# Preln attention on one Trainium2 core: q and k halves copied inside SBUF, chunks placed by hand, three denominator terms, loops written out

## The chip, the cores and the metric

The kernel runs on one core of one Trainium2 chip. The metric is device time in microseconds, from one launch to its end. PE is the tensor engine, DVE the vector engine, ACT the scalar engine, POOL GpSimd, and SP the engine that issues all of this kernel's DMAs.

## What is computed

Eight graphs of 1024 nodes with 512 features; 16 heads of 32.

```python
h = jnp.maximum(_layernorm(x, axis=-1), 0.0)
q, k, v = heads(h @ Wq + bq), heads(h @ Wk + bk), heads(h @ Wv + bv)
scores = jnp.einsum('bhqd,bhkd->bhqk', q, k) * scale
scores = jnp.where(adj[:, None] == 0, -jnp.inf, scores)
attn = jax.nn.softmax(scores, axis=-1)
out = jnp.einsum('bhqk,bhkd->bhqd', attn, v)
x = x + merged(out) @ Wo + bo
```

## The kernel before

A **unit** is four heads (128 of the 512 columns) of one graph; there are four units per graph and 32 in all. A unit has two **sweeps**, each over 512 queries. A sweep has 16 **steps**: eight tiles of 128 keys (kt) by two pairs of heads. So a unit has steps 0 to 31, and "step (2, 19)" is step 19 of a graph's unit 2.

For each step (function `scores`, line 681) PE multiplies a stacked k against a stacked q: q and k are kept as sums of two fp16 halves, high and low, and the four 32-row quarters of a 128-row operand hold (high, low, high, low) of q and (high, high, low, low) of k. One matmul of 128 rows so gives all four products of a head. A step's two score matmuls ("a score pair") are issued one step ahead into one of two pairs of PSUM banks. DVE subtracts the mask into a slot of `ring` (line 905), ACT takes the exponential in place (line 770). `ring` holds four key tiles.

Behind that PE runs **blocks** of four heads, each head on 32 columns of the array: `weighted` (line 694) adds a key tile's probabilities times v to the output (p0 to p7), `denominators` (line 705) adds up the softmax denominators in terms. POOL (`sums`, line 1079) first adds key tiles in pairs and threes into `acc`: kt 0, 1, 2 make term A, kt 3, 4, 5 term B. Key tiles 6 and 7 are terms of their own, straight from `ring`. The table `BLOCKS` says behind which step's scores which blocks stand; numbers of 16 and over run over into the next sweep.

In the space left, PE computes what later units and graphs need, in **chunks** of products that share two PSUM banks in turn: q and k for the next unit (12 products of 512 columns each, line 654), v (48 of 128 columns, line 661), the output projection y of the graph before (12, line 668), the transposes t of the next graph's normalised rows (4, line 650) and the row norms n (line 664) for a check of the fast path. `spread_out` deals a unit's chunks evenly over the steps without blocks, by a cost per product, so a step may end one chunk and begin the next. A chunk's bank is read by ACT (`high`, line 782, after the step in which its products end, then `square`) and by DVE (`low`, line 918, two steps after; `output` for y, `largest_norms` for n).

q's and k's halves lie in `part`. To become stacked operands they go through DRAM: `store_parts` (line 508) writes `part` to `parts`, and `load_stack` (line 513) waits for that and reads it back with four DMAs, one for each quarter, with all four heads.

On ACT, besides: `reciprocal` of the denominators (lines 798, 800, after step 2), `o_high`, `normalise` (line 819) and `to_mask` (line 825). On DVE: `scale_o`, `o_low` (line 960), `statistic` and others. POOL also adds the output bias to x (`bias_x`, line 1087). Each engine's program is written out for graph 0, runs in a hardware loop (`Fori`) over graphs 1 to 6, and is written out for graph 7. Waits are on counts that grow over the whole run. `general_attention` is a second path for other inputs, not run here.

## Time and profile before

| | |
|---|---|
| median of 3 runs | 2086.84 us (2086.14 to 2088.18) |
| the profiled execution | 2085.51 us |
| its span, first to last instruction | 2083.6 us |
| instructions | 40441 |
| PE clock granted, mean | 0.989 of 2.4 GHz |
| DMA | 206.61 MB in 103222 packets |

Times in the rows are microseconds from the start of the span, unless a row says ns. A matmul's end is modelled, so two that follow each other overlap in the timeline; the pitch from start to start is what one costs. "idle before <- X" names what ended an idle time. "x4" means four merged instructions. The chain follows the last instruction back, each time to what released it.

### The profile page before, as it was taken

To read this page: it belongs to the slowest core of one execution; us is meant where nothing else is said; L and a number is where in the kernel's file an instruction comes from. 1 tells how busy PE (TensorE), PEld (TensorE's weight loads), DVE (VectorE), ACT (ScalarE), POOL (GpSimd) and SP (SyncE) were. 2 spreads that over 40 slices of the span, in tenths; PEclk is the share of its full clock that TensorE was granted. 3 is DMA by queue.
4 is the path that set the end of the run, shared out by engine and by line. 5 is a ranking of instruction groups with operands and counts; after the bars stand their busy time and mean duration, and the time that the engine had idled before them with its cause. 6 is when DMAs were issued, how large, how long until landed. Compare 5 with 4: busy or idle time off the path is not lost.

```text
span 2083.6 us, 40441 instructions
## 1 busy us (share of the span) xinstructions
PE 1932.5 (93%) x14336; PEld 776.5 (37%) x14336; DVE 1557.3 (75%) x1587; ACT 1478.1 (71%) x1765; POOL 1302.1 (62%) x581
## 2 busy tenths in 40 slices
PE   3799899998999999999999999999899998999977
PEld 2334344343344333443334333334333343444312
DVE  5688777878768787687867877778767787767773
ACT  3577786677867788668876778767777677866672
POOL 0377567556666567656667557666557566676574
PEclk8999999999999999999999999999999999999999
DMA  5433244342444324343351434424234332442302
GB/s 177 122 87 96 82 112 132 88 107 64 120 112 124 83 76 132 86 122 86 92 142 56 115 93 117 119 74 119 81 109 122 88 106 66 117 122 64 74 1 81
DMA packets 103222, 206.61 MB, mean 99 GB/s; under 512 B 11616, under 2 KB 11744, under 8 KB 103008
## 3 DMA queue, kind: packets, MB, share of 16 engines
q1 hardware_dynamic: 103008, 203.80, 35.2%
q8 instruction: 129, 2.11, 0.4%
...
## 4 chain that ended last, share of the span: by engine, by line
PE 76%; DVE 7%; issue 6%; DMA 5%; ACT 2%; POOL 1%; SPq 1%; DVEq 0%; ACTq 0%; POOLq 0%
PE ps L694 20%; PE ps L681 19%; PE ps L654 15%; PE ps L705 10%; PE ps L668 7%; PE ps L661 6%; DVE ring L905 4%; DMA k_stack<-k_parts 2%; DMA k_parts<-k_part 1%; SPq L513 1%; DMA edges<-adjT 1%; ACT hT_hi L776 1%; DVE k_part L918 1%; POOL acc L1079 1%; ACT ring L770 1%
## 5 line engine op out<-in xcount | busy, mean ns | idle before, releaser
L905 DVE TENSOR_TENSOR ring<-ps,mask 128x1024 f32<-128x1024 f32 x1024 | 1234.6, 1219 | 435.7 <-PE ps L681 399.9
L770 ACT ACTIVATE ring<-ring 128x1024 f32<-128x1024 f32 x1024 | 1069.7, 1051 | 382.9 <-DVE ring L905 374.6
L1079 POOL TENSOR_TENSOR acc<-ring 128x1024 f32<-128x1024 f32 x256 | 604.1, 2371 | 730.2 <-ACT ring L770 729.4
L681 PE MATMUL ps<-q_stack,k_stack 128*128 128x512 f16 x2048 | 610.4, 382 | 85.2 <-DVE ring L905 61.4
L1079 POOL TENSOR_TENSOR acc<-acc,ring 128x1024 f32<-128x1024 f32 x256 | 617.6, 2432 | 0.0
L694 PE MATMUL ps<-ring,v_sb 128*32 128x512 f32 x4096 | 509.1, 604 | 0.0
L681 PEld LDWEIGHTS ps<-q_stack,k_stack 128*128 128x128 f16 x2048 | 157.1, 98 | 481.8 <-DVE ring L905 246.4
L694 PEld LDWEIGHTS ps<-ring,v_sb 128*32 128x32 f32 x4096 | 100.9, 109 | 252.3 <-issue 218.1
L705 PE MATMUL ps<-acc,ones 128*32 128x512 f32 x1024 | 139.8, 597 | 2.7 <-issue 2.6
L705 PE MATMUL ps<-ring,ones 128*32 128x512 f32 x1024 | 137.3, 592 | 0.0
L661 PE MATMUL ps<-wv_hi,hT_hi 128*128 128x128 f16 x1024 | 103.1, 219 | 3.2 <-DVE k_part L918 3.2
L661 PE MATMUL ps<-wv_lo,hT_hi 128*128 128x128 f16 x1024 | 103.2, 219 | 0.0
L825 ACT ACTIVATE mask<-edges,big 128x512 bf16<-128x512 uint32 x120 | 85.4, 711 | 23.1 <-DMA edges<-adjT 23.1
L661 PE MATMUL ps<-wv_hi,hT_lo 128*128 128x128 f16 x1024 | 100.8, 219 | 0.0
L1087 POOL TENSOR_TENSOR x_in<-x_in,bo_row 128x512 f32<-128x512 f32 x56 | 77.7, 1403 | 22.8 <-DMA x_in<-x 22.8
L798 ACT ACTIVATE rden<-ps 128x512 f32<-128x512 f32 x64 | 38.2, 597 | 68.9 <-PE ps L705 68.9
L654 PE MATMUL ps<-hT_hi,wq_hi 128*128 128x512 f16 x256 | 72.7, 388 | 14.2 <-DVE hT_lo L914 14.2
L661 PEld LDWEIGHTS ps<-wv_hi,hT_hi 128*128 128x128 f16 x1024 | 71.4, 98 | 21.9 <-DVE k_part L918 4.2
L668 PE MATMUL ps<-wo_hi,oT_hi 128*128 128x512 f16 x256 | 70.1, 383 | 9.6 <-DVE k_part L918 5.0
L661 PEld LDWEIGHTS ps<-wv_lo,hT_hi 128*128 128x128 f16 x1024 | 71.0, 98 | 14.2
L654 PE MATMUL ps<-hT_hi,wk_hi 128*128 128x512 f16 x256 | 72.5, 379 | 2.1 <-DVE q_part L918 2.1
L654 PE MATMUL ps<-hT_lo,wq_hi 128*128 128x512 f16 x256 | 74.1, 383 | 0.0
...
## 6 DMA issues: line engine op xcount, KB each, us to landing
...
edges<-adjT SPq DMA_DIRECT2D x128, 256.0 KB, 2.9
q_stack<-q_parts SPq DMA_DIRECT2D x128, 256.0 KB, 4.9
k_stack<-k_parts SPq DMA_DIRECT2D x128, 256.0 KB, 5.0
...
```

The lines of the kernel that those rows point to most:

```text
L654: i = nc.tensor.matmul(bank, w[WQ if kind == "q" else WK][:, c, cols], h[:, c, t * HALF:(t + 1) * HALF], start=m == 0, stop=m == 3 * DC - 1)
L661: i = nc.tensor.matmul(bank[:, tt * P:(tt + 1) * P], h[:, c, tok], w[WV][:, c, cols], start=km == 0, stop=km == 3 * DC - 1)
L668: i = nc.tensor.matmul(bank, o[:, c, t * P:(t + 1) * P], w[WO][:, c, :], start=m == 0, stop=m == 3 * DC - 1)
L681: i = nc.tensor.matmul(ps_s(j)[:, hh, :], stack["k"][:, up % 2, h, kt * P:(kt + 1) * P], stack["q"][:, up % 2, h, half * HALF:(half + 1) * ...
L694: i = nc.tensor.matmul(ps[h * DH:(h + 1) * DH, BANK_O, :], v_sb[:, up % 2, kt, h * DH:(h + 1) * DH], head_of(ring[:, slot_of(kt, h // 2), ...
L705: i = nc.tensor.matmul(ps[h * DH:(h + 1) * DH, BANK_D, :], ones[:], head_of(tile, h), start=term == TERMS[0], stop=term == TERMS[-1], tile ...
L770: nc.scalar.activation(tile, tile, ACT.Exp, scale=SCALE / UP / UP).then_inc(s["prob_ready"], 1)
L798: nc.scalar.activation(rden[:], ps[:, BANK_D, :], ACT.Ln).then_inc(s["ln_done"], 1)
L825: nc.scalar.activation(mask[:, kt, half * HALF:(half + 1) * HALF], edges[:, i % EDGE_SLOTS, :].bitcast(U32), ACT.Relu, bias=big[:], scale= ...
L905: nc.vector.tensor_tensor(ring[:, slot_of(kt, pair), :].rearrange("p (a n) -> p a n", n=HALF), ps_s(j), mask[:, kt:kt + 1, half * HALF:(ha ...
L1079: nc.gpsimd.tensor_tensor(acc[:, group, pair, :], first_of, ring[:, slot_of(kt, pair), :], ALU.add).then_inc(s["sum_done"], 1)
L1087: nc.gpsimd.tensor_tensor(tile, tile, bo_row[:], ALU.add).then_inc(s["x_biased"], 1)
```

## The change

1. **Copies.** `parts`, `store_parts` and `load_stack` are gone. `stack_part` copies one half (high or low) of q or k from `part` into the stack with eight DMAs inside SBUF, each of 32 rows of 1024 fp16 values: four heads by two quarters. The high halves are copied once ACT has written both, the low ones once DVE has. Each kind and half has its own semaphore, which ACT and DVE also wait for before they write the next unit's half.
2. **Chunks.** `spread_out` over all chunks is replaced by a table `PRODUCTS`: for each unit, chunk and kind, its first and last step. Only a few steps still hold products of two chunks. The tables `HIGH_AFTER`, `SQUARE_AFTER` and `LOW_AFTER` give for each chunk how many steps after its last product ACT and DVE read it. Statistics, normalising, the biases, masks, `o_high` and `o_low` get new steps; the reciprocal moves from step 2 to 3, `scale_o` from 4 to 5. The last chunk of unit 0 (n) ends in the first step of unit 1.
3. **Terms.** POOL adds kt 0, 1, 2, 3 to term A and 4, 5, 6 to term B; key tile 7 stays a term. There are three terms and ten additions per sweep, where there were four and eight. `BLOCKS` has four groups instead of five.
4. **No loops.** Graphs 1 to 6 are written out on every engine, with constants in the waits.
5. DVE waits for a graph's masks one key tile at a time, where it waited for eight at the head of a sweep.

```diff
-BLOCKS = {6: ("p0", "p1"), 10: ("p2", "p3", "dA"), 14: ("p4", "p5"), 16: ("p6", "dB", "d6"), 18: ("p7", "d7")}
-TERMS = "AB67"
+BLOCKS = {6: ("p0", "p1"), 10: ("p2", "p3"), 14: ("p4", "p5", "dA"), 18: ("p6", "dB", "p7", "d7")}
+TERMS = "AB7"
+SUMMED = {1: 0, 2: 2, 3: 4, 5: 6, 6: 8}
+SUMS = 10
+SUMMED_AT = {"A": 6, "B": 10}
...
-STATS_AT = {(1, 13): 0, (1, 17): 1, (1, 20): 2, (1, 23): 3, (1, 24): 4, (1, 25): 5, (1, 27): 6, (1, 29): 7}
-MEANS_AT, RSTD_AT, SHIFT_AT = (1, 31), (2, 1), (2, 3)
-NORMALISE_AT = {(2, 5): 0, (2, 7): 1, (2, 9): 2, (2, 11): 3, (2, 23): 4, (2, 25): 5, (2, 27): 6, (2, 29): 7}
-T_AT = {(2, 19): 0, (2, 21): 1, (2, 23): 2, (2, 25): 3, (2, 27): 4, (2, 29): 5, (3, 1): 6, (3, 3): 7}
...
+PRODUCTS = [
+    {("q", 0): (0, 3), ("q", 1): (4, 5), ("k", 0): (7, 8), ("k", 1): (8, 11), ("y", 0): (12, 13), ("y", 1): (15, 16), ("v", 0): (17, 20), ("y", 2): (22, 22), ("y", 3): (24, 24), ("y", 4): (26, 28), ("v", 1): (29, 31), ("n", 0): (32, 32)},
...
+LOW_AFTER = [
+    {("q", 0): 2, ("q", 1): 3, ("k", 0): 1, ("k", 1): 2, ("y", 0): 1, ("y", 1): 1, ("y", 2): 1, ("y", 3): 1, ("y", 4): 1, ("n", 0): 1},
...
+STATS_AT = {(1, 13): 0, (1, 18): 1, (1, 21): 2, (1, 23): 3, (1, 25): 4, (1, 27): 5, (1, 28): 6, (1, 30): 7}
+MEANS_AT, RSTD_AT, SHIFT_AT = (1, 31), (2, 0), (2, 4)
+NORMALISE_AT = {(2, 5): 0, (2, 7): 1, (2, 9): 2, (2, 11): 3, (2, 19): 4, (2, 25): 5, (2, 30): 6, (3, 6): 7}
+BIAS_AT = {(0, 4): 0, (0, 7): 1, (0, 10): 2, (0, 11): 3, (0, 22): 4, (0, 26): 5, (0, 30): 6, (1, 1): 7}
+MASK_AT = {3: [17, 18, 21, 22, 24, 26, 28, 30], 0: [1, 3, 5, 7, 8, 9, 10, 12]}
+
+RECIPROCAL_AT, SCALE_O_AT = 3, 5
+O_HIGH_AT, O_LOW_AT = [4, 17, 5, 5], [7, 19, 13, 7]
...
-def spread_out(chunks, slots):
-
-    total = sum(PIECES[kind] * COST[kind] for kind, _ in chunks)
-    plan, spent = {}, 0
-    for kind, t in chunks:
-        for piece in range(PIECES[kind]):
-            runs = plan.setdefault(slots[len(slots) * spent // total], [])
-            if runs and runs[-1][:2] == (kind, t):
-                runs[-1] = (kind, t, runs[-1][2], piece + 1)
-            else:
-                runs.append((kind, t, piece, piece + 1))
-            spent += COST[kind]
+def spread_out(chunk, slots):
+
+    n = PIECES[chunk[2]]
+    cuts = [n * i // len(slots) for i in range(len(slots) + 1)]
+    return {at: (*chunk, a, z) for at, a, z in zip(slots, cuts, cuts[1:]) if a < z}
+
+def chunk_plan():
+
+
+    plan = {}
+    for b in range(B):
+        for up in range(UNITS):
+            for (kind, t), (a, z) in PRODUCTS[up].items():
+                if kind == "y" and b == 0 or b == B - 1 and (kind == "t" or up == UNITS - 1):
+                    continue
+                slots = [j for j in range(a, z + 1) if j % SWEEP not in BUSY] or [a]
+                for at, run in spread_out((b, up, kind, t), [(b * UNITS + up) * TILES + j for j in slots]).items():
+                    plan.setdefault(at, []).append(run)
     return plan
...
-            def store_parts(kind):
-                sp.dma_start(parts[kind], part[kind][:]).then_inc(s[kind + "_stored"], 16)
-
-            def load_stack(U, parity, kind):
-                sp.wait_ge(s[kind + "_stored"], 16 * (U + 1))
-                for quarter, hl in enumerate({"q": (0, 1, 0, 1), "k": (0, 0, 1, 1)}[kind]):
-                    sp.dma_start(stack[kind][quarter * DH:(quarter + 1) * DH, parity, :, :],
-                                 parts[kind][:, hl, :].rearrange("(h p) n -> p h n", h=HG)).then_inc(s["stack_loaded"], 16)
+            def stack_part(U, parity, kind, hl):
+
+                for h in range(HG):
+                    for quarter, which in enumerate({"q": (0, 1, 0, 1), "k": (0, 0, 1, 1)}[kind]):
+                        if which == hl:
+                            sp.dma_start(stack[kind][quarter * DH:(quarter + 1) * DH, parity, h, :], part[kind][h * DH:(h + 1) * DH, hl, :])\
+                                .then_inc(s[f"{kind}_{('high', 'low')[hl]}_stacked"], 16)
 
...
-                        for kind, t in ending_at(up, first, last, j - 3, "qk"):
+                        for c in [c for c in HIGH_AT.get(G - 2, ()) if c[2] in "qk"]:
+                            g, u, kind, t = c
                             if t == 1:
-                                sp.wait_ge(s["low_ready"], chunk_no(SPLIT, b, up, first, (kind, t)) + 1)
-                                store_parts(kind)
-                        for kind, t in ending_at(up, first, last, j - 4, "y"):
-                            sp.wait_ge(stored[t % X_SLOTS], 16 * ((b - 1) * (QT // X_SLOTS) + t // X_SLOTS + 1))
+                                sp.wait_ge(s["high_ready"], chunk_no(SPLIT, c) + 1)
+                                stack_part(unit_no(g, u) + 1, (u + 1) % 2, kind, 0)
+                        for c in [c for c in LOW_AT.get(G - 1, ()) if c[2] in "qk"]:
+                            g, u, kind, t = c
+                            if t == 1:
+                                sp.wait_ge(s["low_ready"], chunk_no(SPLIT, c) + 1)
+                                stack_part(unit_no(g, u) + 1, (u + 1) % 2, kind, 1)
+                        for g, _, kind, t in [c for c in LOW_AT.get(G - 3, ()) if c[2] == "y"]:
...
-            with sp.Fori(1, B - 1) as b:
+            for b in range(1, B - 1):
...
-                    pe.wait_ge(s["stack_loaded"], STACKED * (U + 1))
+                    for kind in "qk":
+                        pe.wait_ge(s[f"{kind}_high_stacked"], STACKED * (U + 1))
+                        pe.wait_ge(s[f"{kind}_low_stacked"], STACKED * (U + 1))
...
-                    if stored_before is not None:
-                        act.wait_ge(s[kind + "_stored"], stored_before)
+                    if stacked_before is not None:
+                        act.wait_ge(s[kind + "_high_stacked"], stacked_before)
...
-                if kt < RING_KT:
-                    if not very_first:
-                        if kt < 2:
-                            dve.wait_ge(s["pv_done"], 8 * V + kt - 3)
-                            dve.wait_ge(s["sum_done"], 8 * V + 2 * kt - 3 + pair)
-                        else:
-                            dve.wait_ge(s["den_done"], len(TERMS) * V + kt - 3)
-                else:
-                    dve.wait_ge(s["pv_done"], 8 * V + kt - 3)
-                    dve.wait_ge(s["sum_done"], 8 * V + {4: 1, 5: 1, 6: 3, 7: 5}[kt] + pair)
+                before = (V - 1, kt + QT - RING_KT) if kt < RING_KT else (V, kt - RING_KT)
+                if not (kt < RING_KT and very_first):
+                    W, k = before
+                    dve.wait_ge(s["pv_done"], QT * W + k + 1)
+                    if k == QT - 1:
+                        dve.wait_ge(s["den_done"], len(TERMS) * (W + 1))
+                    else:
+                        dve.wait_ge(s["sum_done"], SUMS * W + SUMMED[k if k in SUMMED else k + 1] + pair + 1)
...
+                    if stacked_before is not None:
+                        dve.wait_ge(s[kind + "_low_stacked"], stacked_before)
...
-                        if up == 0 and j % SWEEP == 0:
-                            dve.wait_ge(s["mask_ready"], b * 2 * QT + QT * (j // SWEEP + 1))
+                        if up == 0 and j % PAIRS == 0:
+                            dve.wait_ge(s["mask_ready"], b * 2 * QT + j // PAIRS + 1)
...
-                group, k = divmod(kt, 3)
+                group, n = kt // 4, SUMS * V + SUMMED[kt] + pair
                 pool.wait_ge(s["prob_ready"], U * TILES + j + 1)
-                if k == 1 and pair == 0 and not very_first:
+                begins = kt % 4 == 1
+                if begins and pair == 0 and not very_first:
                     pool.wait_ge(s["den_done"], len(TERMS) * (V - 1) + group + 1)
-                if k == 2:
-                    pool.wait_ge(s["sum_done"], 8 * V + 4 * group + pair + 1)
-                first_of = ring[:, slot_of(kt - 1, pair), :] if k == 1 else acc[:, group, pair, :]
+                if not begins:
+                    pool.wait_ge(s["sum_done"], n - 1)
+                first_of = ring[:, slot_of(kt - 1, pair), :] if begins else acc[:, group, pair, :]
```

How the order moves at three places. **PE, graph 0, steps 15 to 19.** L681 (L688 in the change) is a score pair, L694 (L701) four heads' weighted sums with 4 per block, L705 (L712) four heads' denominator term, from `acc` or `ring`; L654 and L661 (L659 and L666) are products for q, k and v. Before:

```order
L681 MATMUL ps<-q_stack,k_stack 128x512 x2
L694 MATMUL ps<-ring,v_sb 32x512 x4
L705 MATMUL ps<-acc,ones 32x512 x4
L705 MATMUL ps<-ring,ones 32x512 x4
L681 MATMUL ps<-q_stack,k_stack 128x512 x2
L654 MATMUL ps<-hT_lo,wk_hi 128x512 x3
L654 MATMUL ps<-hT_hi,wk_lo 128x512
L681 MATMUL ps<-q_stack,k_stack 128x512 x2
L694 MATMUL ps<-ring,v_sb 32x512 x4
L705 MATMUL ps<-ring,ones 32x512 x4
L681 MATMUL ps<-q_stack,k_stack 128x512 x2
```

Now:

```order
L688 MATMUL ps<-q_stack,k_stack 128x512 x6
L666 MATMUL ps<-wv_hi,hT_hi 128x128 x4
L666 MATMUL ps<-wv_lo,hT_hi 128x128 x4
L666 MATMUL ps<-wv_hi,hT_lo 128x128 x4
L666 MATMUL ps<-wv_hi,hT_hi 128x128 x4
L688 MATMUL ps<-q_stack,k_stack 128x512 x2
L701 MATMUL ps<-ring,v_sb 32x512 x4
L712 MATMUL ps<-acc,ones 32x512 x4
L701 MATMUL ps<-ring,v_sb 32x512 x4
L712 MATMUL ps<-ring,ones 32x512 x4
L688 MATMUL ps<-q_stack,k_stack 128x512 x2
```

A group of three blocks (p6, B, 6) and, two steps on, one of two (p7, 7) have become one of four (p6, B, p7, 7); the products of a step are now all of one chunk.

**POOL, graph 0, first additions.** Before, then now:

```order
L1079 TENSOR_TENSOR acc<-ring 128x1024 x2
L1079 TENSOR_TENSOR acc<-acc,ring 128x1024 x2
L1079 TENSOR_TENSOR acc<-ring 128x1024 x2
L1079 TENSOR_TENSOR acc<-acc,ring 128x1024 x2
L1079 TENSOR_TENSOR acc<-ring 128x1024 x2
L1079 TENSOR_TENSOR acc<-acc,ring 128x1024 x2
```

```order
L1087 TENSOR_TENSOR acc<-ring 128x1024 x2
L1087 TENSOR_TENSOR acc<-acc,ring 128x1024 x4
L1087 TENSOR_TENSOR acc<-ring 128x1024 x2
L1087 TENSOR_TENSOR acc<-acc,ring 128x1024 x2
L1087 TENSOR_TENSOR acc<-ring 128x1024 x2
L1087 TENSOR_TENSOR acc<-acc,ring 128x1024 x4
```

Before, a pair of additions that start a sum is followed by one pair that adds to it. Now two pairs follow for term A, one for term B.

**SP, graph 0, from the edges of its second half-masks on.** Before, then now:

```order
L519 DMA edges<-adjT 128x512 x8
L508 DMA q_parts<-q_part 128x2048
L513 DMA q_stack<-q_parts 32x4x1024 x4
L508 DMA k_parts<-k_part 128x2048
L513 DMA k_stack<-k_parts 32x4x1024 x4
```

```order
L518 DMA edges<-adjT 128x512 x5
L512 DMA q_stack<-q_part 32x1024 x8
L518 DMA edges<-adjT 128x512
L512 DMA q_stack<-q_part 32x1024 x8
L518 DMA edges<-adjT 128x512 x2
L512 DMA k_stack<-k_part 32x1024 x16
```

A store and four loads per kind have become sixteen copies, in two eights, and edge loads now stand between them and behind them.

## Rows read from the trace of the kernel before

**Rows 1.** The page, parts 1 and 4: busy us, share, instructions; the chain by engine.
```profile
PE 1932.5 (93%) x14336; PEld 776.5 (37%) x14336; DVE 1557.3 (75%) x1587; ACT 1478.1 (71%) x1765; POOL 1302.1 (62%) x581
...
PE 76%; DVE 7%; issue 6%; DMA 5%; ACT 2%; POOL 1%; SPq 1%; DVEq 0%; ACTq 0%; POOLq 0%
```

**Rows 2.** The chain in order of time, middle of unit 3 to 0: start, us, what.
```profile
688.44 0.43 PE ps L681 x2
688.87 1.29 PE ps L654 x6
```

**Rows 3.** Busy time by engine (instructions): graph 4's first sweep, its sixth, the whole.
```profile
1051.20:1087.30 36.10, 34.52 (x196) 11.91 (x197) 25.97 (x23) 27.68 (x36) 24.59 (x12) 1.00 0.43 120
...
1214.00:1244.20 30.20, 25.18 (x214) 10.31 (x210) 23.43 (x24) 22.50 (x28) 18.74 (x8) 1.00 0.34 87
1051.20:1301.90 250.70, 239.68 (x1792) 96.55 (x1792) 191.57 (x194) 184.50 (x223) 162.85 (x72) 1.00 0.37 102
```

**Rows 4.** The chain again: three blocks, two blocks, the score pair behind, products for v.
```profile
679.56 1.00 PE ps L694 x8
680.56 1.72 PE ps L705 x16
...
692.33 1.85 PE ps L694 x16
694.18 0.54 PE ps L681 x2
...
706.65 1.28 PE ps L661 x23
```

**Rows 5.** PE's timeline in unit 2's second sweep: start, us, line, idle before it.
```profile
983.12 0.60 PE L681 MATMUL ps<-q_stack,k_stack 128*128 128x512 f16 x2 [1.26 <-DVE ring L905]
```

**Rows 6.** POOL's lines 1079 and 1087, one by one: ns min/median/max.
```profile
L1079 POOL TENSOR_TENSOR acc<-acc,ring x256: 2340/2372/3436, 79.5 to 2042.7; 128x1024 f32<-128x1024 f32 x128
...
L1087 POOL TENSOR_TENSOR x_in<-x_in,bo_row x56: 1264/1282/2264, 314.6 to 1869.2; 128x512 f32<-128x512 f32 x56
```

**Rows 7.** PE's timeline at the back edge into graph 4, and out of the loop.
```profile
1048.82 0.61 PE L681 MATMUL ps<-q_stack,k_stack 128*128 128x512 f16 x2
1051.25 0.60 PE L681 MATMUL ps<-q_stack,k_stack 128*128 128x512 f16 x2 [1.83 <-issue]
...
1054.28 0.63 PE L705 MATMUL ps<-acc,ones 128*32 128x512 f32 x3 [0.59 <-issue]
...
1056.12 0.60 PE L681 MATMUL ps<-q_stack,k_stack 128*128 128x512 f16 x2
...
1803.71 1.04 PE L681 MATMUL ps<-q_stack,k_stack 128*128 128x512 f16 x4
...
1807.39 0.61 PE L681 MATMUL ps<-q_stack,k_stack 128*128 128x512 f16 x2
```

**Rows 8.** SP's issues and PE before the first scores.
```profile
49.72 0.33 SPq L508 DMA_DIRECT2D q_parts<-q_part  x1
...
54.89 0.35 SPq L508 DMA_DIRECT2D k_parts<-k_part  x1
...
68.55 1.86 PE L681 MATMUL ps<-q_stack,k_stack 128*128 128x512 f16 x4 [9.45 <-DMA k_stack<-k_parts]
```

**Rows 9.** Lines 513 and 519: issue of stack loads in ns; landing of edge loads.
```profile
L513 SPq DMA_DIRECT2D k_stack<-k_parts x128: 302/432/1437, 61.1 to 1967.7; - x128
...
DMA to landing us min/median/max: 2.4/2.9/7.2
```

**Rows 10.** DVE's line 960, then DVE and POOL at 562 to 568.
```profile
L960 DVE SCALAR_TENSOR_TENSOR oT_lo<-o_raw,b_up,oT_hi x32: 1273/1341/3482, 137.9 to 2052.0; 128x1024 f16<-128x1024 f32 x32
...
564.77 3.13 DVE L960 SCALAR_TENSOR_TENSOR oT_lo<-o_raw,b_up,oT_hi 128x1024 f16<-128x1024 f32 x1
...
562.11 4.71 POOL L1079 TENSOR_TENSOR acc<-acc,ring 128x1024 f32<-128x1024 f32 x2
```

**Rows 11.** Waits: who waited for whom, us in total, times, longest.
```profile
DVE ring L905 <- ACT mask L825: 15.5, 6, 3.3
```

More of the change, by code:

```diff
@@ L267 @@
 UP = 64.0
-STACKED = 16 * 2 * P // DH
+STACKED = 16 * HG * 2
 RING_KT = 4
@@ L753, in _ @@
             graph(0, True, False)
-            with pe.Fori(1, B - 1) as b:
+            for b in range(1, B - 1):
                 graph(b, False, False)
```

204 lines of the change are left out of this document (85 added, 119 removed), and 14 rows, old and new, of tables (HIGH_AFTER, LOW_AFTER, PRODUCTS, SQUARE_AFTER).

## The prediction

> **What bounds the kernel now.** I read the page's busy shares and its chain first [rows 1]: PE 93%, DVE 75%, ACT 71%, POOL 62%, and a chain that is 76% PE. PE's busy time is modelled, so the reader should test it on the chain in order of time [rows 2]: a score pair at 688.44 for 0.43, then six products at 688.87 for 1.29, 0.216 each, with nothing between. Where PE streams like that, only less PE work shortens the kernel. Next, the busy time of one middle graph [rows 3]: 250.7 us from its first masked tile to the next graph's. What PE must do in it, at the pitches of [rows 2, 4]: 128 score pairs x 0.43 = 55, eight sweeps of blocks x 11.4 (next part) = 91, 288 products for q, k and y x 0.216 = 62, 384 narrow ones for v x 0.056 = 21.5, and some 6.5 for transposes and norms: about 236 to 238. So PE idles 13 to 14 us per graph. Of that, 3.6 is the loop's edge (part 2), and 5 lie in the second sweep of unit 2 alone (25.18 busy of 30.20 [rows 3]), where PE stands up to 1.26 us before a score pair until DVE has masked a tile [rows 5]. DVE is the second limit, in light stretches only.
>
> **1. The denominator terms: -69 us.** Each of the 64 sweeps has 12 blocks of four heads now (8 weighted sums, 4 terms) in five groups. In the chain three blocks in a row take 1.00 + 1.72 = 2.72 us (679.56 to 682.27) and two take 1.85 (692.33 to 694.18) [rows 4]: 0.87 per block, 0.11 per group, and the score pair behind a group takes 0.54 instead of 0.43, another 0.11. The change makes it 11 blocks in four groups: 0.87 + 0.22 = 1.09 less, x 64 = 69. PE streams around most of them, so all of it counts; where DVE sets the pace, in light sweeps, a block is still on the path, because the next score pair queues behind it on PE. POOL takes the term over: two adds more per sweep, 128 x 2.4 = 307 us [rows 6]. In the middle graph POOL goes from 162.85 [rows 3] to 201 of some 240. The worst place is the first sweep of unit 0, with four biases: from tile 2's exponential on (about 5 us in), 10 adds x 2.4 + 4 biases x 1.3 [rows 6] end 34 us in; PE wants term B at step 18, behind 31.6 us of steps, two free ones, a score pair and one block: 36 us. Covered, at 0. If the cover goes, it is the third rival.
>
> **2. The loops: -18 us.** Two score pairs and the three blocks between them take 1048.82 to 1056.12 = 7.30 us at a back edge, with 1.83 and 0.59 us that end in "issue", no wait. The same work where graph 6 leaves the loop takes 1803.71 to 1807.39 = 3.68 [rows 7]. Five back edges x 3.6 = 18. Bounds: 12 (the two gaps alone, 2.42 x 5) and 18. I count 0 for fetching seven graphs of straight code: graphs 0 and 7 are straight already, and PE streams in them as well (3.68 us for 3.6 of work [rows 7]).
>
> **3. q and k straight into the stacks: -3 us.** This chain is on the path only at the start: the q store at 49.72, the k store at 54.89, PE standing 9.45 us until 68.55 [rows 8]. Now 16 copies for q and 16 for k go through SP. The issue of a small copy has no row; between 0.3 (the shortest stack load) and 0.43 (their median [rows 9]) I take 0.43, as these lie back to back like those: 16 x 0.43 = 6.9. q's fill SP from 49.7 to 56.6, k's to 63.5; the last lands 2.4 to 2.9 later [rows 9], at 66: 2.5 to 3 us earlier. Bounds: 0, and -9.45, all of PE's wait. Inside the graphs the low half of k comes last, in unit 2 after step 25: 8 x 0.43 + 2.9 = 6.3 us, while the score pair that waits is six steps, over 10 us, away. 0; if that slack went, each unit would start late (fourth rival). Queued behind the copies on SP are the edges for the masks of unit 0 at steps 9 and 10, behind eight copies each (3.4 us). ACT, 27.68 busy of 36.10 there [rows 3], may stand up to 2.6 us once per graph; PE takes its exponentials two tiles or more late, so most of that is absorbed: +3 in all, bounds 0 and +21.
> The Trainium skill speaks against these copies (SBUF — State Buffer, The DMA setup-cost knee): every transfer carries a fixed cost of about 2 us, mostly completion, and transfers of 64 KiB run at about 138 GB/s, 30% of the best. By that rule, as an estimate, the megabyte for k takes 7.6 us and this part is worth about 2 instead of 3. No row shows a transfer of 64 KiB between two places in SBUF.
>
> **4. Own steps for each chunk: 0.** This moves work and removes none. I added up PE's and DVE's work step by step, from the durations above and DVE's 1.22 per tile. Better: transposes now stand between fuller steps (today a step of 0.43 alternates with one of 0.9 while DVE has two instructions in each pair). Worse: with longer groups PE's other steps shrink to 1.1 to 1.3 us, at DVE's 1.22 and its gap or under, and extras land there: the shift at (2, 4) before a step of 0.43, four statistics in the light steps 23 to 28 of unit 1. Both come to 10 to 12 us of PE idle per graph, edge left out. So 0, bounds -6 and +6 per graph.
>
> **5. DVE and POOL hold each other up: +12 us.** The low half of o (two SBUF inputs) takes 1.28 to 1.34 us mostly, but 3.13 once per graph; at 564.77, 2.05 of it pass until the POOL adds beside it end at 566.82, and 1.08 remain [rows 10]. Today three of four meet POOL idle or at an add's last moment. With POOL busy 84% instead of 65%, in longer rows, and the halves now after tiles 7, 19, 13 and 7, I let each wait half an add, 1.2: 32 x 1.2 less today's 8 x 1.85 is +23 on DVE, half of it on the path. Bounds 0 and +52 (each waits 2.1).
>
> **6. Masks by key tile: -4 us.** DVE waits 15.5 us in six places for the last mask of a graph [rows 11], but PE streams through the one at 1803.71 [rows 7]. Its worth is 0 to -1 per graph: -0.5 x 8.
>
> **Sum.** -69 - 18 - 3 + 3 + 0 + 12 - 4 = -79. The profiled execution took 2085.51 us around a span of 2083.6; the median of the runs, 2086.84, lies 1.3 above it. So 2006.5 on the first, 2007.8 on the second; I say **2007**.
>
> **The rivals.** *PE's idle falls too* (0.12): part 4 gives back half of the 12 us per graph and part 5 costs nothing, 2007 - 48 - 12 = 1947 to 1985. For: today's idle is clumped [rows 3, 5]. Against: the light steps above.
> *DVE becomes the pace* (0.10). Groups of 2, 2, 3 and 4 blocks with their score pair take 2.4, 2.4, 3.2 and 4.1 us, and DVE can mask one tile in each, done 1.76 after its start (0.53 for the scores, 1.23). It idles 5.1 per sweep; 191.57/8 = 24 busy [rows 3], 1.4 of gaps and 5.1 are 30.5. With waits for ACT, 246 per graph against today's 248 without the edge: 16 + 18 + 3 gained, 2050 (to 2065). For: the group of four is new. Against: half of DVE's extras stand right behind groups, where it idles anyway.
> *POOL becomes the bound* (0.02), the slower side. 80 adds and 10 us of biases per graph fill 251 us once an add takes 3.0; at 3.2 it is 266, + 15 x 8 = 120, less 21 of parts 2 and 3: 2186. For: some adds take 3.4 [rows 6]. Against: the median of 256 is 2.37, and five DVE instructions per graph can stretch one.
> *The copies come late* (0.02). If the small ones were served in turn at 1.5 us, k's sixteen take 24 us where 17 to 19 are left in units 1 to 3: 6 x 24 = 144, less 79 + 3: 2075 to 2151. For: a landing takes 2.4 us at least [rows 9]. Against: no row shows copies of one queue served in turn.
>
> **Numbers.** The forecast has 0.74, with 1985 to 2030 as its own range. Mine reaches into the first two rivals: 1975 to 2045. Faster by over 0.2% (4 us, about what a measurement of this kernel can tell): forecast and first two rivals, 0.96; within 0.01; slower 0.03.
>
> **What would show it.** Right: term blocks down by a quarter; middle graphs of 240 us; no gap at a graph's edge; POOL at 1610 busy; first score at 66; copies of 0.3 to 0.45 on SP; low halves of o near 2.5. Wrong: PE standing for DVE over 15 us per graph, low halves at 1.3, term B waiting for POOL, or PE waiting for a stack.

## The result and the profile after

The changed kernel is slower. Its median over ten runs is 2102.65 us (2091.54 to 2105.43), that of the kernel before in the same series 2086.34 (2084.56 to 2088.22); the ratio is 1.007, 95% interval 1.0054 to 1.0085. The forecast was 2007, with 1975 to 2045 as its range. The profiled execution took 2105.36 us, 19.9 more than that of before.

The page of the changed kernel, its span, parts 1 and 4, answers to [rows 1]:

```profile
span 2103.5 us, 35729 instructions
...
PE 1903.8 (91%) x13824; PEld 780.2 (37%) x13824; DVE 1554.9 (74%) x1587; ACT 1481.7 (70%) x1765; POOL 1605.2 (76%) x709
...
PE 51%; SPq 18%; DVE 11%; issue 7%; ACT 6%; DMA 5%; POOL 2%; DVEq 0%; POOLq 0%; ACTq 0%
SPq L512 16%; PE ps L701 14%; PE ps L688 13%; DVE ring L911 9%; PE ps L659 8%; PE ps L673 6%; PE ps L712 5%; PE ps L666 4%; ACT ring L776 3%; DMA edges<-adjT 2%; ACT mask L831 1%; POOL acc L1087 1%; SPq L518 1%; PE ps L655 1%; DMA x_in<-x 1%
```

PE does less: 512 matmuls fewer, as forecast, and 29 us less of busy time. But the chain has a new member. SP, 1% of it before, has 18%, and 16% are one line: the issue of the copies (L512). PE's part fell from 76% to 51%. The waits say who stands for them:

```profile
ACT mask L831 <- DMA edges<-adjT: 105.6, 38, 4.8
...
PE ps L688 <- DVE ring L911: 67.7, 84, 3.4
...
PE ps L688 <- DMA k_stack<-k_part: 27.0, 11, 13.1
```

(total, times, longest; before, ACT's wait for edges was 23.1 us.) Now the copies themselves, line 512 in the trace, duration of an issue in ns, minimum, median, maximum:

```profile
L512 SPq DMA_DIRECT2D q_stack<-q_part x512: 507/591/2077, 47.9 to 1986.8; - x171
L512 SPq DMA_DIRECT2D k_stack<-k_part x512: 507/591/1838, 58.7 to 1998.5; - x171
...
DMA to landing us min/median/max: 1.9/2.0/3.8
```

A copy lands fast, 2.0 us, but holds SP for 0.59 us, not for the 0.43 of a stack load [rows 9], and they follow at a pitch of 0.63. SP's timeline before the first scores of graph 4 (start, us, times):

```profile
1039.05 0.33 SPq L518 DMA_DIRECT2D edges<-adjT  x1
1039.43 5.17 SPq L512 DMA_DIRECT2D q_stack<-q_part  x8
1044.65 0.57 SPq L518 DMA_DIRECT2D edges<-adjT  x1
1045.27 4.95 SPq L512 DMA_DIRECT2D q_stack<-q_part  x8
1050.26 0.58 SPq L518 DMA_DIRECT2D edges<-adjT  x1
1050.89 5.12 SPq L512 DMA_DIRECT2D k_stack<-k_part  x8
1056.05 0.58 SPq L518 DMA_DIRECT2D edges<-adjT  x1
1056.67 4.94 SPq L512 DMA_DIRECT2D k_stack<-k_part  x8
```

For 22.6 us SP does nothing but issue; an edge load gets its turn every 5.6 us. ACT stands for the next ones, and PE for ACT (ACT's and PE's timeline, in brackets the idle time before):

```profile
1053.54 0.72 ACT L831 ACTIVATE mask<-edges,big 128x512 bf16<-128x512 uint32 x1 [2.40 <-DMA edges<-adjT]
...
1059.43 0.72 ACT L831 ACTIVATE mask<-edges,big 128x512 bf16<-128x512 uint32 x1 [3.28 <-DMA edges<-adjT]
...
1061.15 1.06 PE L701 MATMUL ps<-ring,v_sb 128*32 128x512 f32 x8 [2.94 <-ACT ring L776]
```

The second place is the start of unit 3. SP, then PE:

```profile
1235.23 5.85 SPq L512 DMA_DIRECT2D k_stack<-k_part  x8
1241.13 0.58 SPq L504 DMA_DIRECT2D x_in<-x  x1
1241.75 4.94 SPq L512 DMA_DIRECT2D k_stack<-k_part  x8
...
1248.35 0.59 PE L688 MATMUL ps<-q_stack,k_stack 128*128 128x512 f16 x2 [1.92 <-DMA k_stack<-k_part]
```

What follows costs more than the 1.92. Stretches of 1.5 us, columns as in [rows 3]; the third number from the end is the granted clock:

```profile
1247.00:1248.50 1.50, 0.15 (x1) 0.13 (x2) 0.00 (x0) 1.50 (x3) 1.50 (x1) 1.00 0.56 85
1248.50:1250.00 1.50, 1.27 (x20) 0.59 (x18) 0.92 (x1) 0.21 (x1) 0.75 (x1) 1.00 0.38 138
1250.00:1251.50 1.50, 0.45 (x3) 0.48 (x4) 1.50 (x4) 1.06 (x1) 0.00 (x0) 0.78 0.00 0
1251.50:1253.00 1.50, 1.50 (x6) 0.82 (x6) 0.86 (x2) 0.83 (x2) 0.00 (x0) 0.50 0.04 11
1253.00:1254.50 1.50, 1.50 (x5) 0.55 (x4) 1.50 (x2) 0.71 (x1) 0.00 (x0) 0.58 0.66 175
1254.50:1256.00 1.50, 1.50 (x15) 0.42 (x16) 1.01 (x2) 1.06 (x1) 0.21 (x1) 1.00 0.00 0
```

After PE had stood 1.92 us, worked 1.3 and stood again (0.15 and 0.45 busy of 1.5 in the first and third rows), it ran at the lower of its two levels, 1.2 GHz, for over 3 us. The next long stop begins 17 us behind the second one's end: the low half of o (L968) starts just behind a POOL addition and takes 3.36 us, PE stands 2.51, and the clock drops again:

```profile
1266.27 2.36 POOL L1087 TENSOR_TENSOR acc<-acc,ring 128x1024 f32<-128x1024 f32 x1
1266.35 3.36 DVE L968 SCALAR_TENSOR_TENSOR oT_lo<-o_raw,b_up,oT_hi 128x1024 f16<-128x1024 f32 x1
...
1270.90 0.66 PE L688 MATMUL ps<-q_stack,k_stack 128*128 128x512 f16 x2 [2.51 <-DVE ring L911]
```

```profile
1271.50:1274.00 2.50, 2.50 (x11) 0.99 (x13) 2.29 (x4) 2.50 (x5) 0.42 (x1) 0.50 0.22 36
```

The two places lie in one sweep, unit 3's first. In graph 4 it took 28.28 us before, and takes 35.12 now; the whole graph takes 252.9 where it took 250.7 [rows 3], though PE is busy 4.6 us less. Before, then now:

```profile
1244.24:1272.52 28.28, 26.57 (x169) 9.20 (x170) 23.20 (x24) 22.23 (x26) 19.74 (x8) 1.00 0.16 52
```

```profile
1249.07:1284.19 35.12, 31.07 (x221) 13.37 (x218) 27.44 (x26) 23.61 (x29) 23.91 (x11) 0.90 0.15 46
1064.00:1316.90 252.90, 235.08 (x1730) 97.35 (x1729) 191.66 (x195) 185.35 (x223) 201.96 (x89) 0.98 0.31 85
```

PE's stop for k's stack is not the copies' alone, though. In the changed kernel such stops add up to 27.0 us, 13.1 of them ahead of the first scores; with the stacks still through DRAM (e4 below) they are 37.7 with 9.4 ahead. What the copies add is ACT's wait for edges: 105.6 us where e4 has 32.4.

### The profile page after: what moved, and what is told of

It reads as the page before. It is cut to its first block, busy times and chain, and to the rows that moved or that the text cites. A ratio compares the mean times of both kernels' runs of the same rounds, so it can differ in the third digit from the quotient of the medians.

```text
span 2103.5 us, 35729 instructions
## 1 busy us (share of the span) xinstructions
PE 1903.8 (91%) x13824; PEld 780.2 (37%) x13824; DVE 1554.9 (74%) x1587; ACT 1481.7 (70%) x1765; POOL 1605.2 (76%) x709
## 4 chain that ended last, share of the span: by engine, by line
PE 51%; SPq 18%; DVE 11%; issue 7%; ACT 6%; DMA 5%; POOL 2%; DVEq 0%; POOLq 0%; ACTq 0%
SPq L512 16%; PE ps L701 14%; PE ps L688 13%; DVE ring L911 9%; PE ps L659 8%; PE ps L673 6%; PE ps L712 5%; PE ps L666 4%; ACT ring L776 3%; DMA edges<-adjT 2%; ACT mask L831 1%; POOL acc L1087 1%; SPq L518 1%; PE ps L655 1%; DMA x_in<-x 1%
## 5 line engine op out<-in xcount | busy, mean ns | idle before, releaser
L1087 POOL TENSOR_TENSOR acc<-ring 128x1024 f32<-128x1024 f32 x256 | 614.2, 2419 | 434.1 <-ACT ring L776 433.2
L1087 POOL TENSOR_TENSOR acc<-acc,ring 128x1024 f32<-128x1024 f32 x384 | 916.5, 2413 | 31.7 <-ACT ring L776 31.5
L688 PE MATMUL ps<-q_stack,k_stack 128*128 128x512 f16 x2048 | 620.2, 389 | 97.9 <-DVE ring L911 67.7
L701 PE MATMUL ps<-ring,v_sb 128*32 128x512 f32 x4096 | 524.7, 617 | 37.2 <-ACT ring L776 36.8
L688 PEld LDWEIGHTS ps<-q_stack,k_stack 128*128 128x128 f16 x2048 | 163.6, 99 | 460.7 <-DVE ring L911 237.6
L701 PEld LDWEIGHTS ps<-ring,v_sb 128*32 128x32 f32 x4096 | 108.0, 111 | 316.5 <-issue 209.9
L831 ACT ACTIVATE mask<-edges,big 128x512 bf16<-128x512 uint32 x120 | 85.6, 713 | 105.6 <-DMA edges<-adjT 105.6
L712 PE MATMUL ps<-acc,ones 128*32 128x512 f32 x1024 | 140.4, 621 | 4.4 <-POOL acc L1087 4.4
L666 PE MATMUL ps<-wv_hi,hT_hi 128*128 128x128 f16 x1024 | 99.4, 220 | 0.0
L666 PE MATMUL ps<-wv_hi,hT_lo 128*128 128x128 f16 x1024 | 99.2, 219 | 0.0
L666 PE MATMUL ps<-wv_lo,hT_hi 128*128 128x128 f16 x1024 | 99.2, 219 | 0.0
L666 PEld LDWEIGHTS ps<-wv_hi,hT_hi 128*128 128x128 f16 x1024 | 73.9, 98 | 31.3 <-issue 0.6
L926 DVE SCALAR_TENSOR_TENSOR k_part<-ps,b_up,k_part 128x512 f16<-128x512 f32 x64 | 47.5, 743 | 49.6 <-ACT k_part L788 49.2
L659 PE MATMUL ps<-hT_hi,wq_hi 128*128 128x512 f16 x256 | 72.6, 410 | 6.3 <-DVE hT_lo L920 6.3
L968 DVE SCALAR_TENSOR_TENSOR oT_lo<-o_raw,b_up,oT_hi 128x1024 f16<-128x1024 f32 x32 | 72.1, 2254 | 1.2 <-ACT oT_hi L812 1.2
L659 PE MATMUL ps<-hT_hi,wk_hi 128*128 128x512 f16 x256 | 65.8, 379 | 6.7 <-DVE q_part L926 6.7
L666 PEld LDWEIGHTS ps<-wv_lo,hT_hi 128*128 128x128 f16 x1024 | 69.1, 98 | 5.7
L666 PEld LDWEIGHTS ps<-wv_hi,hT_lo 128*128 128x128 f16 x1024 | 69.1, 98 | 5.7
```

The source lines that it names most:

```text
L659: i = nc.tensor.matmul(bank, w[WQ if kind == "q" else WK][:, c, cols], h[:, c, t * HALF:(t + 1) * HALF], start=m == 0, stop=m == 3 * DC - 1)
L666: i = nc.tensor.matmul(bank[:, tt * P:(tt + 1) * P], h[:, c, tok], w[WV][:, c, cols], start=km == 0, stop=km == 3 * DC - 1)
L688: i = nc.tensor.matmul(ps_s(j)[:, hh, :], stack["k"][:, up % 2, h, kt * P:(kt + 1) * P], stack["q"][:, up % 2, h, half * HALF:(half + 1) * ...
L701: i = nc.tensor.matmul(ps[h * DH:(h + 1) * DH, BANK_O, :], v_sb[:, up % 2, kt, h * DH:(h + 1) * DH], head_of(ring[:, slot_of(kt, h // 2), ...
L712: i = nc.tensor.matmul(ps[h * DH:(h + 1) * DH, BANK_D, :], ones[:], head_of(tile, h), start=term == TERMS[0], stop=term == TERMS[-1], tile ...
L831: nc.scalar.activation(mask[:, kt, half * HALF:(half + 1) * HALF], edges[:, i % EDGE_SLOTS, :].bitcast(U32), ACT.Relu, bias=big[:], scale= ...
```

## The experiments

Theory: the copies hold SP, and what stands behind them or waits for their last is late; a second loss is DVE's low half beside POOL's additions; the clock makes both dearer. Rivals: the new places of the chunks, POOL's load, or less to be had from terms and loops. All medians of experiments are of four runs, with the kernel before at 2087 to 2089 in the same series; the changed kernel's is the one above.

### The change taken apart: e1 to e4

e1: in the kernel before, on all five engines

```diff
-            with pe.Fori(1, B - 1) as b:
+            for b in range(1, B - 1):
```

> The kernel before with graphs 1 to 6 written out and nothing else changed. Theory (the back edge costs 3.6 us, five times): 18 us less, 2066 to 2071, and the stretch from graph 3's last scores to graph 4's first as short as at the way out of the loop, 3.7 us for 7.3. Rival (straight code has to be fetched, and that shows where PE is tight): no gain, 2083 to 2095.

e2: e1 with `BLOCKS`, `TERMS`, `SUMMED` and the waits of the change. As step 16 has no blocks now, `spread_out` puts products there, so the chunks move a little too.

> e1 with the three denominator terms and their ten additions, old stacks through DRAM, old places of the chunks. Theory (PE is the pace, so the 16 blocks fewer per graph pair count in full): e1 less 55 to 69, about 2000 to 2015. Rival 1 (POOL at 80% and its lock with DVE eat it): e1 less 30 or less, low halves of o near 2.5 us each. Rival 2 (DVE is the pace once the groups are four): about 2035, PE waiting over 15 us per graph for DVE.

e3: e2 with `stack_part` in place of `store_parts` and `load_stack`, high halves at the chunk's end + 2, low ones at + 3.

> e2 with q and k copied inside SBUF by 64 small copies per unit pair instead of a store and four loads, at the old places. Theory (SP is held 0.63 us by each copy, 20 us per unit, and the loads of edges behind them come late): slower than e2 by 15 to 60 us, ACT waiting for edges 80 us or more in all where e2 has some 25. Rival (the copies do no harm where the chunks stand at their old places, and the loss comes from the new places): within 5 us of e2.

e4: the changed kernel with the DRAM way put back:

```diff
-                                stack_part(unit_no(g, u) + 1, (u + 1) % 2, kind, 1)
+                            store_parts(c[2])
...
+                        for g, u, kind, _ in [c for c in LOW_AT.get(G - 3, ()) if c[2] in "qk" and c[3] == 1]:
+                            load_stack(unit_no(g, u) + 1, (u + 1) % 2, kind)
```

> The changed kernel with the stacks built through DRAM as before, all else as changed. Theory (the copies on SP cost 8 us at the start of unit 3 and 4 to 5 us at a graph's edge, eight graphs): 2103 less 90 to 100, 2000 to 2015, with the first sweep of unit 3 at 28 us instead of 36. Rival (the new places, DVE held up by POOL, or the lower granted clock are to blame): 2080 to 2105, the first sweep of unit 3 still over 33 us.

| kernel | us | ratio to before, 95% interval | step |
|---|---|---|---|
| before | 2087.08 | | |
| e1 | 2076.19 | 0.9944 (0.9926 to 0.9962) | loops out: -11 |
| e2 | 2042.17 | 0.9792 (0.9768 to 0.9815) | three terms: -34 |
| e4 | 2053.32 | 0.9842 (0.9804 to 0.9879) | new places, masks by tile: +11 |
| changed | 2102.65 | | copies: +49 |
| e3 | 2144.97 | 1.0285 (1.0262 to 1.0307) | copies at the old places: +103 on e2 |

e4's four runs lie between 2045 and 2060, so its +11 is only just clear of noise. The copies turn a gain of 34 us into a loss of 16. At the old places they cost twice as much: there ACT waits 88.7 us for edges, in 14 waits of up to 6.9, and behind it PE waits 34.8 us for DVE's half of k and 26.4 for ACT's exponentials, up to 5.4 at a time.

Where the 49 lie: the profiled executions of the changed kernel and e4 are 56 us apart. Counted from sweep to sweep, 31 of it stand in the first and last sweeps of the graphs, where the edges are loaded, 16 in unit 3's first sweep and 3 ahead of the first scores.

No step came out as forecast. e4's first sweep of unit 3 is still too long (34.99 us at a clock of 0.90), so rival and theory are each half right there.

### What it is about the copies: e9, e12, e6, e5, e8

e9: in e4, each load of a kind is cut into four, one per head: sixteen transfers of the copies' shape, but from DRAM.

```diff
-                    sp.dma_start(stack[kind][quarter * DH:(quarter + 1) * DH, parity, :, :],
-                                 parts[kind][:, hl, :].rearrange("(h p) n -> p h n", h=HG)).then_inc(s["stack_loaded"], 16)
+                    for h in range(HG):
+                        sp.dma_start(stack[kind][quarter * DH:(quarter + 1) * DH, parity, h, :], parts[kind][h * DH:(h + 1) * DH, hl, :])\
+                            .then_inc(s["stack_loaded"], 16)
```

> e4 (changed kernel, stacks through DRAM) with each of the four loads of a kind cut into four, one per head: sixteen loads of 32 rows by 1024 from DRAM, the shape of the direct copies. Theory (what SP pays is the number of small transfers, whatever they read): issue 0.59 us each as for the copies, and the time goes from e4's 2053 to 2095 to 2130, the stack later still than with copies since a store comes first. Rival (the dear thing is a transfer from SBUF to SBUF; loads of this shape cost SP 0.3 to 0.45): 2053 to 2070.

2134.83 us, +82 on e4, 5 above the theory's range. Line 514 of e9:

```profile
L514 SPq DMA_DIRECT2D q_stack<-q_parts x512: 302/421/1995, 50.8 to 2020.3; - x171
```

The time went the theory's way, the price the rival's: from DRAM the same shape holds SP 0.42 us, from SBUF 0.59. Both ways sixteen of them (7 to 10 us of SP) are too many. The two losses are not the same, however: in e9 a store comes first, so PE's stops for k's stack rise from e4's 37.7 us to 79.9 and ACT's wait for edges from 32.4 to 73.5, while with the copies only the second rises. So e9 shows that many small transfers cost much from DRAM as well; it does not show how the copies' 49 divide between their number and their source.

e12: the changed kernel with unit 3's low half of o moved (as e7 below), and k's copies issued by ACT.

> The changed kernel with the low half of o moved as in e7 and k's copies issued by ACT, q's by SP, at the same steps. Theory (a copy holds the engine that issues it for 0.6 us, so ACT, with 184 us of 250 busy, pays 38 us more per graph and its exponentials come late): slower than the changed kernel with SP alone, 2110 to 2160. Rival (ACT only hands them over, 0.1 us each, and two queues take the copies in half the time): 2030 to 2055.

2145.60 us, within the theory's range. e12 differs from e15 below (2065.63) in nothing but who issues k's copies, so this costs 80 us. ACT's queue in e12, then ACT behind it:

```profile
L504 ACTq DMA_DIRECT2D k_stack<-k_part x496: 514/612/1818, 101.5 to 2043.5; - x166
```

```profile
1072.25 5.67 ACTq L504 DMA_DIRECT2D k_stack<-k_part  x8
1077.96 0.72 ACT L831 ACTIVATE mask<-edges,big 128x512 bf16<-128x512 uint32 x1 [4.68 <-issue]
```

The price is paid by whoever issues: 0.61 us each on ACT, whose own work stops 4.68 us for eight; its stops that end in "issue" before exponentials, 90.1 us in all, are new.

e6: same copies, but taken from a list, at most three per step, behind the step's other transfers.

```diff
-                            sp.dma_start(stack[kind][quarter * DH:(quarter + 1) * DH, parity, h, :], part[kind][h * DH:(h + 1) * DH, hl, :])\
-                                .then_inc(s[f"{kind}_{('high', 'low')[hl]}_stacked"], 16)
+                            pending.append((stack[kind][quarter * DH:(quarter + 1) * DH, parity, h, :], part[kind][h * DH:(h + 1) * DH, hl, :],
+                                            s[f"{kind}_{('high', 'low')[hl]}_stacked"], None))
...
+                        copy_some(3)
```

> The changed kernel with the same 32 copies per unit, but SP issues at most three of them per step, behind what else that step asks of it (edges, x, outputs); within the units nothing else is changed. Theory (copies in blocks of eight hold SP for 5 us each, and the edges behind them come late, ACT stands for them in order): ACT's waits for edges fall from 106 us to under 40, the first sweep of a graph from 36 to about 32, in all 20 to 35 us less, 2068 to 2083; unit 3's start stays late or gets later by up to 2 us. Rival (the order on SP does not matter, the price is the number of copies in flight or their traffic): within 5 us of 2103.

e5: in the changed kernel, unit 2's last k chunk two steps earlier (`PRODUCTS`), and one `NORMALISE_AT` later for it.

```diff
-    ... ("t", 1): (18, 19), ("k", 1): (20, 23), ("t", 2): (24, 24), ...
+    ... ("k", 1): (19, 21), ("t", 1): (23, 23), ("t", 2): (25, 25), ...
...
-    ... (2, 25): 5, ...
+    ... (2, 28): 5, ...
```

> The changed kernel with unit 2's last k chunk moved ahead of transposes 1 and 2 (its last products in step 21, not 23), so that its sixteen copies start two steps, 3.7 us, earlier. Theory (in the changed kernel the sixteen copies of k take 10.1 us on SP from step 25 and land after PE has reached unit 3's first scores; PE stands 2 us for them, and its clock falls to half for 3.4 us more): the wait for k's copies in unit 3 goes, 2 to 4 us per graph, 2070 to 2088. Rival (the stall there is DVE's and POOL's, the copies only happen to end beside it): 2098 to 2108.

e8: e5, e6 and e7 together.

> The changed kernel with the three mends of e5, e6 and e7 together, direct copies kept. Theory (three separate losses, each in its own place): 2103 less the sum of what the three give singly, 2030 to 2055, so that the direct copies are no worse than DRAM. Rival (SP stays too busy with 20 us of copies in a unit of 60, the late ones only move): over 2070.

Both single mends made it worse: e6 2128.54 us, e5 2117.19. Both lie outside theory and rival. ACT's wait for edges in e6 fell to 24.8, as expected, but PE now stands 93.5 us in all for k's stack, here 7.21 before graph 4's first scores (line 701 of e6); in e5 the wait for k went, and ACT stands for a row of x whose load was queued behind k's sixteen copies. SP (the last nine of the sixteen) and ACT in e5, then PE in e6:

```profile
1251.49 6.24 SPq L512 DMA_DIRECT2D k_stack<-k_part  x9
1257.77 8.93 SPq L504 DMA_DIRECT2D x_in<-x  x4
1260.71 0.81 ACT L825 ACTIVATE x_in<-x_in,shift,rstd 128x512 f32<-128x512 f32 x1 [5.62 <-DMA x_in<-x]
```

```profile
1080.68 1.87 PE L701 MATMUL ps<-q_stack,k_stack 128*128 128x512 f16 x4 [7.21 <-DMA k_stack<-k_part]
```

My prices for them failed, since I counted only the wait that each removes. e8 came to 2078.78, outside its 2030 to 2055, the rival's case. Of the 24.2 us from 1039.05 to the next unit's first scores at 1063.27, 20 go to a unit's 32 copies; in these runs another order moved the wait from edges to stack to x and did not remove it. e15 below, without e5 and e6, is 13 us faster than e8.

### DVE beside POOL: e7, e15, e13

e7 is e4, e15 the changed kernel, each with one number changed:

```diff
-O_HIGH_AT, O_LOW_AT = [4, 17, 5, 5], [7, 19, 13, 7]
+O_HIGH_AT, O_LOW_AT = [4, 17, 5, 5], [7, 19, 13, 19]
```

> e4 (changed kernel, stacks through DRAM) with the low half of o of unit 3's step 7 moved to step 19, where POOL has just run out of additions. Theory (there it starts beside a POOL addition, takes 3.37 us for 1.34, PE runs dry behind it and is given half its clock for 3.4 us): each such low half takes 1.3 us, the first sweep of unit 3 falls from 33.6 by 2 to 4 us, in all 15 to 30 us less than e4's 2053. Rival (the light sweep waits for the stack or for DVE's other work, and hides this): within 5 us of e4, with the low half short all the same.

> The changed kernel with nothing but unit 3's low half of o moved from step 7 to 19. Theory (the lock and the clock behind it are a loss of their own, the same 27 us as between e4 and e7): 2103 less 20 to 30, 2073 to 2083, so that the direct copies, and not the lock, are 60 to 75 us of the distance to e11. Rival (unit 3 waits for its stack anyway, and hides it): 2095 to 2103.

e7 took 2026.76 us, 27 less than e4, as the theory had it, and e15 2065.63 us, 37 less than the changed kernel and more than the 20 to 30 expected. The moved low half takes 1.28 us in both, and unit 3's first sweep of graph 3, e4 and then e7:

```profile
973.34:1006.77 33.43, 29.38 (x220) 12.73 (x217) 27.45 (x26) 24.75 (x31) 25.05 (x11) 0.95 0.18 55
```

```profile
962.39:991.63 29.24, 27.71 (x220) 12.28 (x217) 23.97 (x26) 24.52 (x31) 23.07 (x11) 1.00 0.21 64
```

4.2 us less: the low half's 3.4 have left this sweep (1.28 of them now stand in the next), and the clock stayed full. An estimate from the rows: e4's PE stood 2.51 us behind this low half, as in the changed kernel, and a mean clock of 0.95 over 33.43 us means 3.3 us at half speed, which lose 1.7; 2.5 and 1.7 are the 4.2. No run takes the clock's part away by itself.

With this low half out of the way, e15 against e7 gives the price of the copies again: 39 us, of which 27 stand in the graphs' first and last sweeps and 2 in unit 3's first. The 16 us there between the changed kernel and e4 need the misplaced low half as well.

e13: e1 with unit 2's low half two steps later.

```diff
-                        if j == o_high_at(up, first) + 2 and not (first and up == 0):
+                        if j == (9 if up == 2 else o_high_at(up, first) + 2) and not (first and up == 0):
```

> e1 (kernel before, written out) with the low half of o in unit 2 two steps later, in a gap between POOL's additions. Theory (the loops did cost 18 us, and e1 gave only 11 because that low half now meets POOL: 3.5 us for 1.28, unit 2's first sweep 33.0 us for 31.6): 2076 less 8 to 10, 2066 to 2069, the sweep at 31.6. Rival (writing out costs 7 us somewhere else, such as fetching code): 2073 to 2079.

2065.77 us, as expected, and the sweep takes the 31.6 expected. In e1 that low half took 3.51 us, in e13 1.27:

```profile
1188.70 3.51 DVE L960 SCALAR_TENSOR_TENSOR oT_lo<-o_raw,b_up,oT_hi 128x1024 f16<-128x1024 f32 x1
```

```profile
1192.25 1.27 DVE L960 SCALAR_TENSOR_TENSOR oT_lo<-o_raw,b_up,oT_hi 128x1024 f16<-128x1024 f32 x1
```

In the kernel before, too, this low half takes 1.27 us in the middle graphs. So the loops were worth 21 us, and their removal let one low half per graph meet a POOL addition, which gave 10 of it back.

### The terms: e10, e16, e14

e10: e2 with the group of four split. e16: e2 with step 16 kept free of products.

```diff
-BLOCKS = {6: ("p0", "p1"), 10: ("p2", "p3"), 14: ("p4", "p5", "dA"), 18: ("p6", "dB", "p7", "d7")}
+BLOCKS = {6: ("p0", "p1"), 10: ("p2", "p3"), 14: ("p4", "p5", "dA"), 16: ("p6",), 18: ("dB", "p7", "d7")}
```

```diff
-SLOTS = [j for j in range(1, 29) if j % SWEEP not in BUSY]
+SLOTS = [j for j in range(1, 29) if j % SWEEP not in BUSY | {0}]
```

> e2 (old places, written out, three terms, through DRAM) with the group of four blocks split: one block behind step 16's scores, three behind step 18's, so groups of 2, 2, 3, 1 and 3, and the chunks back in the very steps of e1. Theory (behind the long group PE stands for DVE, which has but two tiles to mask meanwhile, and that is part of what the terms failed to give): PE's waits for DVE fall from 107 us towards e1's 68, and in spite of 14 us more of group changes the time is 2020 to 2040. Rival (the waits come from the light steps, whose work shrank, not from the group): 2045 to 2060.

> e2 with step 16 kept free of products, so that its chunks stand where e1 and e10 have them and only the groups differ: 2, 2, 3 and 4 blocks here, 2, 2, 3, 1 and 3 in e10. Theory (the group of four is what makes PE stand for DVE, and that eats the 14 us of its one group change less): equal to e10 within 5 us, 2038 to 2048, PE's waits for DVE 25 us or more above e10's 79. Rival (the chunks in step 16 were to blame in e2): 2025 to 2033, the waits at 80.

e10 took 2042.73 us, e16 2064.13. PE's waits for DVE in e1, e2, e10 and e16, one line of each:

```profile
PE ps L681 <- DVE ring L905: 68.2, 90, 2.5
```

```profile
PE ps L685 <- DVE ring L907: 106.8, 115, 2.5
```

```profile
PE ps L685 <- DVE ring L907: 78.8, 91, 2.2
```

```profile
PE ps L685 <- DVE ring L907: 108.8, 116, 2.3
```

e10's waits fell as the theory said, its time did not: 2042.73 lies between the two ranges and is that of e2. With the products in the same steps, the group of four costs 21 us more than one and three blocks, though it spares PE 64 x 0.22 = 14: it loses 35. e16's waits are those of the theory, its time is in neither range; both had it at 2048 or less. That products in step 16 (e2) win 22 us while the waits stay at 107 is not explained by the waits; unit 2's low half takes 1.36 us in e2 and 3.46 in e10 and e16, which is a part of it, how large stays open.

e14: e11 (below) with four terms, five groups and eight additions, as before the change.

> e11 with four denominator terms in five groups and eight additions per sweep, as before the change; all else as e11. Theory (the new places leave DVE less to do behind groups, so here the third term saved gives more than the 34 us of e2 against e1): e11 plus 45 to 69, 2056 to 2080. Rival 1 (DVE takes half of it back at any places): plus 25 to 40, 2036 to 2051. Rival 2 (POOL, freer with eight additions, gives something back): plus 20 or less.

2103.77 us, 93 more than e11, above every case and above PE's own 69. The 93 are not of the terms alone: a group in step 16 also pushes products out of it here, and two low halves per graph now take 2.98 and up to 2.36 us where e11 has 1.27 and 1.34. What the fourth term itself costs at the new places stays open.

### The version that beats both: e11

e11: e7 with the loads of a stack one step earlier (`LOW_AT.get(G - 2, ())` for `G - 3`).

> e7 with the loads of a stack one step earlier on SP, right behind the store. Theory (in e7 PE stands 30 us in all for k's stack at units' starts, and its clock falls behind that): 10 to 25 us less than e7's 2027, 2002 to 2017. Rival (SP now stands inside the store's landing, and the edges behind it come late): 2025 to 2040.

2011.10 us, 16 less than e7, as the theory had it; ratio to before 0.9638 (0.9612 to 0.9665). A middle graph:

```profile
1017.20:1257.60 240.40, 231.71 (x1729) 96.88 (x1728) 188.51 (x195) 184.98 (x224) 200.09 (x88) 0.99 0.38 106
```

The graph of 240 us of the forecast exists, without the copies. Against this version the copies (e15) cost 55 us, 5 short of the 60 to 75 expected. So their price is 39 to 55 us by three comparisons: 49 (e4), 39 (e7), 55 (e11).

## Why the prediction was wrong

**Part 3, the copies, is the step that failed**: "0" inside the graphs and +3 for ACT, measured +49 (39 to 55). The main thing is ACT's wait for edges. The masks were each put behind one block of eight (3.4 us), in unit 0 only, "2.6 us once per graph"; but an issue is 0.59 and not 0.43, which came from loads out of DRAM, its pitch is 0.63, and the four blocks of a unit follow each other with one edge load between them. So ACT stood 2.40 and 3.28 already at the end of unit 3, and again in unit 0: 105.6 us in the whole run, where e4 has 32.4. PE did not absorb it; it stood 2.94 behind the second.

A smaller thing is the last half of k, given "8 x 0.43 + 2.9 = 6.3 us" against over 10. The high half's eight copies stand right ahead of the low's, so k's copies run from 1235.23 to 1246.7, and a landing takes 2 us: 13.1 us from the first issue to the scores, and PE stood 1.92. But e4 stands there too (1.75 in graph 4), so this is no price of the copies against DRAM.

The fourth rival named PE's wait for its stack, which is not where the loss against e4 lies, and a mechanism that did not occur: it asked for copies served in turn at 1.5 us, and they follow each other at 0.63. That the measured time lies in its range, 2075 to 2151, is luck. The prediction had the queue on SP as +3 only, with +21 as its upper bound.

The prologue went the other way too. The first scores came at 70.35, not 66, 1.8 us later than before [rows 8]:

```profile
70.35 1.87 PE L688 MATMUL ps<-q_stack,k_stack 128*128 128x512 f16 x4 [13.12 <-DMA k_stack<-k_part]
```

By the Trainium skill's rule that the prediction weighed (SBUF — State Buffer, The DMA setup-cost knee), a megabyte in pieces of 64 KiB takes 7.6 us; measured are sixteen pitches of 0.63 and a landing of 2.0, 12.1 us. The rule's fixed cost of 2 us is what a landing takes here; its 138 GB/s are not reached (64 KiB in 0.63 us are 104). So the rule spoke against the change rightly, and was still too kind.

**Part 1, the terms**: -69 forecast (1.09 x 64 is 70), -34 at the old places (e2), and only -24 against e13, whose low half is as short as e2's. With the chunks left where they were it is -12 (e16). "All of it counts" failed: PE's waits for DVE rose by 39 us. The second rival named this (a group of four with one tile for DVE to mask), and e16 against e10 puts 35 us to it. It is not all: e10, with five groups, still gives 33 where its 64 blocks less should give 64 x 0.87 = 56. That part stays open. POOL covered its additions in the graphs, as said: PE stood 4.4 us for them in all and DVE 23.1 (8.5 before). But 3.3 of PE's are at the end, where nothing is left to hide them; from the last masked tile to the end it is 47.8 us now and was 39.7. The chain of the changed kernel passes through a last addition there (key tile 6) that the kernel before had not:

```profile
2058.66 2.35 POOL acc L1087
2061.01 0.04 issue
2061.05 1.94 PE ps L712 x8
```

**Part 2, the loops**: -18, with 12 to 18 as bounds; -11 alone, -21 with the low half out of POOL's way (e13). The mechanism was right: in e1 the same two score pairs and three blocks at the edge into graph 4 take 3.68 us (1044.42 to 1048.10), for 7.30. The size lies 1 below its bounds in e1 and 3 above them in e13.

**Part 5, DVE and POOL**: mechanism right, +12 forecast. In the changed kernel one misplaced low half per graph is worth 37 us (e15), within the bound of 52. The average of half an addition hid what matters: two of four meet an addition and wait 2.1 or near it, two don't, and the one in a light sweep also costs the clock. No part of the prediction had the clock in it. The mean granted fell from 0.989 to 0.965; as an estimate, that is some 147 us at half speed in the changed kernel for 46 before, (1 - 0.965) x 2 of the span and (1 - 0.989) x 2. How much of it cost time no run shows.

**Parts 4 and 6**, 0 and -4, can only be measured with part 5's +12, since e4 has the new places of the low halves too: forecast +8 together, measured +11 (e4 against e2). That they agree is luck. The 11 hold 27 of one low half (e7) and 16 of late loads of a stack (e11), which the new places had left short of time; without both, the new places are worth -31 (e11 against e2), within part 4's bounds of 6 a graph and on the side of the first rival.

The steps, -11 - 34 + 11 + 49 = +15, give the 16 between the medians by construction. They are the prices in this order; in another order a step can come out otherwise, as the copies do (+49 and +103).
